# A state-space convolution with routed low-rank update: kernel numbers split into high and low parts before the skew, blocks reversed in time

## What is computed

```
P = dtA[:, :, None] * arange(L);  Cs = Cc * (exp(dtA) - 1) / A
K = 2 * Re(einsum('hn,hnl->hl', Cs, exp(P)))
y = irfft(rfft(u * mask) * rfft(K))[..., :L] + (u * mask) * D[:, None]
y = y * mask
```

## Time and profile before

| | us |
|---|---|
| runs | 608.7, 608.7, 610.63 |
| median | 608.7 |
| the profiled execution | 609.9 |
| its span in the profile | 608.1 |
| PE busy | 581.6 (96% of the span) |
| PEld, DVE busy | 529.0, 490.3 |
| POOL, ACT busy | 385.9, 317.2 |

### The profile page before, as it was taken

The page is one execution under the profiler, slowest core; times in us unless marked ns, Lnnn a source line. Parts: engine busy times, 40 slices in busy tenths (PEclk is TensorE's granted clock), DMA queues, the critical chain, the costliest instruction groups (busy, mean ns, idle before and its releaser), DMA issues.

```text
span 608.1 us, 13318 instructions
## 1 busy us (share of the span) xinstructions
PE 581.6 (96%) x3617; PEld 529.0 (87%) x3617; DVE 490.3 (81%) x1371; ACT 317.2 (52%) x1059; POOL 385.9 (63%) x520
## 2 busy tenths in 40 slices
PE   3589999999999999999999999999999999999996
PEld 3478999999999989999999999999999999999984
DVE  7768888887888888788888888888888888887875
ACT  3666754555465455546545554664555456445420
POOL 4668657666765766676575667657566765665430
PEclk9999999999999999999999999999999999999999
DMA  6212454454345344434534443453444345445422
GB/s 119 73 54 86 149 155 98 144 155 125 120 148 156 100 141 153 125 119 148 157 96 143 153 135 110 148 157 97 143 152 132 114 147 157 102 139 151 138 85 83
DMA packets 37582, 77.64 MB, mean 128 GB/s; under 512 B 12476, under 2 KB 20862, under 8 KB 37510
## 3 DMA queue, kind: packets, MB, share of 16 engines
q1 hardware_dynamic: 28358, 43.76, 28.8%
q10 hardware_dynamic: 9152, 33.03, 13.3%
HBM read 43.16 MB, written 33.62 MB: 126 GB/s over the span
## 4 chain that ended last, share of the span: by engine, by line
PE 92%; DVE 3%; ACT 2%; issue 1%; POOL 1%; DMA 0%; ACTq 0%; POOLq 0%
PE psYo L1060 20%; PE psZ L1080 19%; PE psO L1060 15%; PE psYe L1060 13%; PE psS L1060 11%; PE psO L1107 5%; PE psXe L1071 5%; PE psXo L1071 5%; PE psZ L1136 1%; DVE psS L918 0%; DVE ex L758 0%; DMA logs<-in_L_cond_log_dt_dram 0%; POOL both L465 0%; DVE ost L957 0%; ACT L577 0%
## 5 line engine op out<-in xcount | busy, mean ns | idle before, releaser
L504 POOL TENSOR_TENSOR Slo<-Sf,Shi 128x384 fp32r<-128x384 f32 x64 | 65.3, 1021 | 166.1 <-ACT Shi L651 166.1
L918 DVE SCALAR_TENSOR_TENSOR psS<-Sf,tab,psS 64x128 f32<-64x128 f32 x256 | 91.9, 359 | 48.1 <-ACT Sf L646 41.2
L1080 PE MATMUL psZ<-Wt,Y 128*128 128x136 f32 x1024 | 129.2, 279 | 0.0
L1080 PEld LDWEIGHTS psZ<-Wt,Y 128*128 128x128 f32 x1024 | 123.3, 190 | 0.1
L646 ACT ACTIVATE Sf<-psS 128x128 f32<-128x128 f32 x64 | 17.8, 277 | 200.3 <-PE psS L1060 200.3
L957 DVE TENSOR_TENSOR ost<-psO,xt 128x512 f32<-128x512 f32 x128 | 87.7, 690 | 1.2 <-PE psO L1060 1.1
L497 POOL TENSOR_TENSOR Xlo<-xeven,Xhi 128x512 fp32r<-128x512 f32 x64 | 82.9, 1295 | 0.0
L465 POOL TENSOR_TENSOR both<-coarse,fine 128x512 f32<-128x512 f32 x64 | 69.0, 1079 | 1.3 <-ACT fine L591 1.2
L941 DVE TENSOR_TENSOR wlo<-psZ,whi 128x128 fp32r<-128x128 f32 x64 | 18.7, 292 | 41.2 <-ACT whi L656 41.2
L1060 PE MATMUL psYo<-Xhi,Thi 128*128 128x512 f32 x128 | 51.2, 400 | 0.0
L1060 PE MATMUL psYo<-Xlo,Thi 128*128 128x512 f32 x128 | 51.1, 399 | 0.0
(11 more groups left out here) (193 smaller groups left out, 1522.2 us busy)
## 6 DMA issues: line engine op xcount, KB each, us to landing
xt<-in_x_dram SPq DMA_DIRECT2D x64, 512.0 KB, 4.9
out_dram<-ost ACTq DMA_DIRECT2D x63, 512.0 KB, 5.1
Traw<-kdram SPq DMA_DIRECT2D x64, 128.0 KB, 2.9
kdram<-krow SPq DMA_DIRECT2D x64, 1.0 KB
A_nat<-in_L_ffn_A_dram SPq DMA_DIRECT2D x1, 512.0 KB, 5.1
B_nat<-in_L_ffn_Bw_dram SPq DMA_DIRECT2D x8, 64.0 KB, 3.5
out_dram<-ost SPq DMA_DIRECT2D x2, 256.0 KB, 2.0
lens_i<-in_itok_B_dram SPq DMA_DIRECT2D x1, 64.0 KB, 5.0
```

The source lines that it names most:

```text
L504: pool.tensor_tensor(Slo[h.s2][:, :], Sf[h.s2][:, :], Shi[h.s2][:, :].bitcast(F32), ALU.subtract).then_inc(slo_done, 1)
L918: dve.scalar_tensor_tensor(psS[to, new], Sf[h.s2][fr, old], tab2[fr, BR, h.n:h.n + 1], psS[to, new], ALU.mult, ALU.add).then_inc(brought_d ...
L1080: last = pe.matmul(psZ[:, 0:NW], Y[:, j, c, :], Wt[:, 2 * c + j, :], start=(j == 0 and c == 0), stop=(j == 1 and c == NE - 1), skip_group_ ...
```

## The change

K is split into hi and lo while it is still two columns (`k_split`, ACT), all four columns are transposed, two DMAs write them into two rows of DRAM, and one DMA reads both, skewed, into one tile `T` (128x2x256, four buffers), which PE loads as it is. `t_hi` and `t_lo` are gone. Since nothing reads the skewed numbers backwards any more, the positions of the outputs stand reversed inside each block of 128. `g_hi` and `g_lo` read `Grev` forwards and `from_states` takes the halves of G the other way round, the mask counts positions downwards, and the weights of `project` are reversed once in the setup: `A_rev` by a copy on POOL, `route_rev` by one on ACT.

```diff
-        zeros = sb("zeros", [1, P])
+        zeros = sb("zeros", [2, P])
+        A_rev = sb("A_rev", [P, NB, P])
+        route_rev = sb("route_rev", [E, NB, P])
...
             def write_kernel(h):
                 need(sp, k_turned, h.n + 1)
                 need(sp, t_in[h.s2], h.half * 16)
-                sp.dma_start(bass.AP(kdram.tensor, h.s2 * (P + Q), [[G32, P // G32], [P, 2], [1, G32]]),
-                             krow[h.s2][0:P:G32, :, :]).then_inc(k_out[h.s2], 16)
+                for part in range(2):
+                    sp.dma_start(bass.AP(kdram.tensor, (h.s2 * 2 + part) * (P + Q),
+                                         [[G32, P // G32], [P, 2], [1, G32]]),
+                                 krow[h.s2][0:P:G32, part, :, :]).then_inc(k_out[h.s2], 16)
...
             def skew_kernel(h):
-                need(sp, thi_done, h.n - 1)
-                need(sp, tlo_done, h.n - 1)
-                need(sp, k_out[h.s2], h.half * 16 + 16)
-                sp.dma_start(Traw[h.s2][:, :],
-                             bass.AP(kdram.tensor, h.s2 * (P + Q), [[1, P], [1, Q]])
+                need(sp, y_mm, (h.n - 3) * 2)
+                need(sp, k_out[h.s2], h.half * 32 + 32)
+                sp.dma_start(T[h.s4][:, :, :].bitcast(F32),
+                             bass.AP(kdram.tensor, h.s2 * 2 * (P + Q), [[1, P], [P + Q, 2], [1, Q]])
                              ).then_inc(t_in[h.s2], 16)
...
+            pool.wait_ge(in_A, 16)
+            pool.tensor_copy(A_rev[:, :, :],
+                             A_nat[:, :].rearrange("p (c l) -> p c l", l=P)[:, :, ::-1]).then_inc(rev_done, 1)
             pool.wait_ge(g_set, 6)
             pool.wait_ge(tab_done, 1)
...
-            def t_hi(h):
-                need(act, t_in[h.s2], h.half * 16 + 16)
-                need(act, y_mm, (h.n - 1) * 2)
-                act.activation(Thi[h.s2][:, :, :].rearrange("p a b -> p (a b)"), Traw[h.s2][:, ::-1],
-                               ACT.Copy).then_inc(thi_done, 1)
+            def k_split(h):
+                need(act, kraw_done, h.n * 2 + 2)
+                need(act, k_turned, h.n - 1)
+                act.activation(kcol[h.s2][:, 0, :, 0:1], kraw[h.s2][:, :].rearrange("p (j a) -> p j a", a=1),
+                               ACT.Copy).then_inc(khi_done, 1)
+                need(act, khi_done, h.n + 1)
+                for j in range(2):
+                    act.activation(kcol[h.s2][:, 1, j, 0:1], kcol[h.s2][:, 0, j, 0:1].bitcast(F32), ACT.Identity,
+                                   scale=-1.0, bias=kraw[h.s2][:, j:j + 1]).then_inc(klo_done, 1)
...
             x_even(first[0])
+            act.wait_ge(in_rw, 16)
+            act.activation(route_rev[:, :, :], route_nat[:, :].rearrange("p (c l) -> p c l", l=P)[:, :, ::-1],
+                           ACT.Copy).then_inc(rev_done, 1)
             act.wait_ge(tabs_turned, 1)
...
             def turn_k(h):
-                need(dve, kcol_done, h.n * 2 + 2)
+                need(dve, klo_done, h.n * 2 + 2)
...
                 if head(2).there:
+                    b_lo(head(2))
                     turn_k(head(2))
-                    b_lo(head(2))
...
             def within(h, j):
-                need(pe, thi_done, h.n + 1)
-                need(pe, tlo_done, h.n + 1)
-                T = [(Thi[h.s2][:, j, :], Tlo[h.s2][:, j, :]) for j in range(2)]
+                need(pe, t_in[h.s2], h.half * 16 + 16)
+                K = [(T[h.s4][:, 0, j * P:(j + 1) * P], T[h.s4][:, 1, j * P:(j + 1) * P]) for j in (1, 0)]
...
-            pe.wait_ge(in_A, 16)
-            pe.wait_ge(in_rw, 16)
+            pe.wait_ge(rev_done, 2)
```

More of the change, by code:

```diff
@@ L521, in step @@
                     g_table(head(3))
-                if head(1).there:
-                    t_lo(head(1))
                 if head(3).there:
@@ L540, in _ @@
             angle_steps(parts[1])
-            t_lo(first[0])
             g_lo(first[1])
@@ L548, in _ @@
             weigh(parts[1])
-            t_lo(first[1])
             g_lo(first[3])
@@ L597, in g_hi @@
                 need(act, y_mm, (h.n - 3) * 2)
-                act.activation(Ghi[h.s4][:, :], Grev[h.s2][:, ::-1], ACT.Copy).then_inc(ghi_done, 1)
+                act.activation(Ghi[h.s4][:, :], Grev[h.s2][:, :], ACT.Copy).then_inc(ghi_done, 1)
             def m_matrix(h):
@@ L669, in step @@
                     b_hi(head(2))
+                    k_split(head(2))
                 if head(0).there:
@@ L673, in step @@
                     x_even(head(1))
-                    t_hi(head(1))
                 if head(3).there and not is_head(head(0), 1):
@@ L720, in _ @@
             b_hi(first[0])
+            k_split(first[0])
             g_hi(first[0])
@@ L726, in _ @@
             b_hi(first[1])
-            t_hi(first[0])
+            k_split(first[1])
             s_hi(first[0])
@@ L733, in _ @@
             b_hi(first[2])
+            k_split(first[2])
             g_hi(first[2])
@@ L736, in _ @@
             m_matrix(first[3])
-            t_hi(first[1])
             g_hi(first[3])
@@ L1119, in within @@
                 need(pe, y_masked, h.n * 2 - 1 + j)
[L1120 removed]
+                three(psY[j][:, :], [(K[0], X[j])] + [(K[1], X[0])] * j, True, False)
             def from_states(h):
@@ L1127, in from_states @@
                 for j in range(2):
-                    G = tuple(g[h.s4][:, j * P:(j + 1) * P] for g in (Ghi, Glo))
+                    G = tuple(g[h.s4][:, (1 - j) * P:(2 - j) * P] for g in (Ghi, Glo))
                     three(psY[j][:, P:512], [(G, (Shi[h.s2][:, :], Slo[h.s2][:, :]))],
@@ L1183, in _ @@
             turn_tables(pack1, psY[0], 4)
-            pe.wait_ge(in_A, 16)
-            pe.wait_ge(in_rw, 16)
+            pe.wait_ge(rev_done, 2)
             for c in range(NB):
                 cols = slice((c % 4) * P, (c % 4 + 1) * P)
-                pe.transpose((psO[1] if c // 4 else psZ)[:, cols], A_nat[:, c * P:(c + 1) * P], ident[:, :])
+                pe.transpose((psO[1] if c // 4 else psZ)[:, cols], A_rev[:, c, :], ident[:, :])
             for c in range(NB):
-                last = pe.transpose(psS[:, c * E:(c + 1) * E], route_nat[:, c * P:(c + 1) * P],
+                last = pe.transpose(psS[:, c * E:(c + 1) * E], route_rev[:, c, :],
                                     ident[0:E, 0:E])
```

49 lines of the change are left out of this document (21 added, 28 removed).

## The result

| | before | changed |
|---|---|---|
| median of the runs, us | 608.7 | 612.88 (612.22 to 613.07, four runs) |
| ratio | | 1.0059, interval 1.0038 to 1.0080 |
| the profiled execution, us | 609.9 | 613.03 |
| its span, us | 608.1 | 611.2 |
| PE, PEld, DVE busy, us | 581.6, 529.0, 490.3 | 583.0, 531.6, 493.9 |

The changed kernel is slower by 0.6%. POOL lost 43 us of work and PE gained nothing from it. The time, 612.9, lies outside the predicted range (607.2 to 611.3).

What follows compares the result with a forecast made beforehand. PE's own work was taken to bound the loop, its waits being single and in the setup. Terms 1.3 - 0.4 - 0.2 = +0.7 gave 610.6 for the profiled execution, less 1.2 = 609.4 us; range 607.2 to 611.3.

Steps and rivals of the forecast that it cites:

- 0 in all, never below 0: Loop: work taken off POOL and ACT gains nothing, the added work stays hidden from PE; 0 us, never a gain.
- The change gives PE the same matmuls of the same shapes: Loop: PE's matmuls keep shapes and order, so the loop can only lose, by making PE wait; no size beyond 0.
- The copy of A, +1.3: Setup: POOL's copy holds up DVE's chain of exponentials by about its own length; +1.3 us, ends 0 and +2.5.
- The first head, -0.4: First head: T lands without Thi and Tlo, so PE starts at 32.6 instead of 33.06; -0.4 us, ends -1.8 and +0.5.
- DVE now makes Blo first: Loop: DVE makes Blo, then transposes 128 columns instead of 64, perhaps 0.1 us more, covered by 0.64 us idle.
- The second head, -0.2: Second head: Thi and Tlo leave the queues of ACT and POOL, so the wait for gated values shortens by 0.2 us.
- The race at the first table: Setup: POOL's table starts before DVE's rho and is not held, giving back 0.9 us: 608.5; chance 0.16.
- rival 2: Setup: the copy of A costs DVE nothing, starting later or not holding it: 608.1 us; chance 0.10.
- Rival 3: Setup: the copy takes the two-input price of 2.5 us and the first head wins nothing: 611.2 us; chance 0.13.
- Rival 4: Loop: a split of 1.1 us or longer delays Shi past its slack; each further 0.1 us costs 6 us; chance 0.04.
- Rival 5, the clock: First head: after a shorter pause PE's clock might rise before 33 us, saving up to 2.4: 607.0 us; chance 0.07.
- From the profiled execution to the median, -1.2: Whole kernel: the profiled execution's 1.2 us above the median of 608.7 is taken off the forecast at the end.

Runs made afterwards that it cites:

- run 2: Changed kernel with Blo made before K's transpose in the setup's first three heads, and A reversed on ACT instead of POOL: 610.44 us, ratio 1.0016.
- run 1: Changed kernel with Blo made before the transpose of K's columns for the first three heads of the setup: 611.25 us, ratio 1.0034.
- run 13: Kernel before, whole, with 79 groups of 12 matmuls appended after its last product, moving operand addresses; first mark at 49.07 us, no total time given.
- run 8: Changed kernel with Blo first, A reversed on ACT, tiles at 64-byte multiples, and Mx and first state ahead of the second head's sines: 610.81 us.
- run 12: Changed kernel with Blo first, A reversed on ACT, kraw padded, plus six one-column ACT operations behind the split in each loop head: 657.07 us.
- runs 7 and 15: Changed kernel with Blo first and A reversed on ACT; then all tiles at 64-byte multiples (609.2 us), or kraw padded and operands 32 bytes off (609.72).
- run 4: Changed kernel with kraw padded from 2 to 16 columns: 609.83 us (one run).
- run 3: Kernel before with two unused tiles of the size of A_rev and route_rev: 609.26 us (one run).
- run 10: Kernel before with two unused two-column tiles where the changed kernel has kraw: 610.84 us, ratio 1.0016.

## Why the prediction was wrong

**The loop, "0 in all, never below 0": wrong, by 1.6 us.** The argument went over the waits, and every point of it held: no repeated wait, Shi in time, T hidden, whi and wlo in time (wlo ends at 307.27 and PE loads the first operand of `up` at 307.36, 0.09 us later, where it was 0.07). The first step that failed stands in front of it: "The change gives PE the same matmuls of the same shapes", from which their length was taken to be the same. It depends on where the operands lie too, and the change had moved them. It could also have gone the other way: with kraw at 16 columns the loop would have been 0.8 us shorter than before, so "never below 0" was wrong as well. No row shows this; the last sentence of the prediction's signs ("matmuls of another length in the loop than now") names it only as what would prove it wrong.

**The copy of A, +1.3: the mechanism right, the size 0.95.** DVE stood still under POOL's copy, as under Xlo in the earlier trace rows, and ACT's copy in run 2 takes the cost away. A copy of 1024 columns took 1.11 us, less than half the price by columns of Xlo (2.5) and less than the halved 1.3. The Trainium skill (GPSIMD Engine Reference, Performance versus the Vector engine) gives 1.8 cycles an element as the best case, 1.5 us as an estimate; the measured 1.11 is below it, and it decides.

**The first head, -0.4: the gain and its eater were both missed.** PE's `within` started at 33.07 against 33.06. Taking off the 0.95 of the copy, which comes first, the head won 0.94 and not 0.4, since T landed 3.1 us after its issue and not 3.6. But `bring`, which goes ahead of `within`, had become 0.79 us later. This is the second step that failed. "DVE now makes Blo first" is said of the loop, where it is so; in the setup the code keeps `turn_k` ahead of `b_lo`, and `turn_k` now waits for the split. The split's 0.7 us were counted on the way of T and not for who stands behind `turn_k` on DVE, so the sum has no term for Blo. The delay passed down to the states and the next inputs (2.0 us for Mx, 1.6 for issue), and by run 1 it was worth 1.55 us at the first mark. The first mark was late by 0.81 where the sum had +0.7, but that was luck: the profiled execution of the kernel before ran its first head at the pace of 1.2 GHz and the changed one at 2.4. Against run 13, the kernel before at 2.4, the changed kernel's mark is late by 2.2 us (51.31 against 49.07).

**The second head, -0.2.** One wait for the gated values (1.3 us) went, and others took its place; run 8 shows how they are handed on.

**Rivals.** The race at the first table didn't flip: the changed kernel has rho at 21.78 and POOL's table at 21.82 with 1.97 us, both 1 us later. The copy did cost, which ends rival 2. Rival 3's price for the copy (2.5) was too high; its time (611.2) came nearest and is still 1.7 us too low, for another reason. Rival 4 stayed away, with 0.5 us to spare, and is real beyond that (run 12). Rival 5, the clock: PE indeed worked at 2.4 GHz from 33.07 on (0.39 us for a product that took 0.63 until 36.61 before), and the gain was lost to the waits behind. But the shorter pause is not shown to be the cause: with the full pause of 1.84 us run 13 ran fast there too, and with pauses of 0.95 and 0.86 runs 7 and 15 ran slow. In the stretch from 42 to 50 us, after waits of 1.55 and 1.95 us, the granted clock was 0.79:

```profile
42.00:50.00 8.00, 7.40 (x37) 6.99 (x38) 4.98 (x16) 6.82 (x27) 4.93 (x10) 0.79 0.32 100
```

and the 16 products of the projection at 43.25 took 3.55 us instead of 2.0. In run 4 they took 2.0 after waits of 1.03 and 1.95 us.

**From the profiled execution to the median, -1.2.** The third step that failed: "I take the 1.2 off at the end" takes what the kernel before's profiled execution had above its median for something that the changed kernel's has as well. That one was only 0.15 us above its median, so this added 1.05 us to the difference of the medians. The spans of the kernel before, over all comparisons, lie in two groups, 606.7 to 607.1 and 607.7 to 608.4 us, and the profiled one is of the upper. The slow first head, worth 1.0 to 1.4 us at the first mark (50.50 against 49.51 in run 3 and 49.07 in run 13), is of the size of that distance and would explain it; the executions that make the median have no trace, so this is not shown.

**In sum**, 4.2 us against the forecast's 0.7, by the profiled executions: 1.6 from the step's length (not foreseen), 0.1 more in the setup (0.81 for 0.7), 0.7 from the clock at the end and 1.05 from the step to the medians. With the first heads at the same clock it reads otherwise: 1.6 from the step and 1.5 more than forecast in the setup (2.2 for 0.7, which is what Blo's place costs in run 1), which leaves 0.4 for the end and the rest.

**Small signs.** POOL's busy time fell to 342.7 (forecast about 340). ACT's did not fall by something but rose by 12.6 us: the split shows 0.72 us a head where Thi had 0.41. T landed after 3.8 us in the median (3.6), and x after 5.7 instead of 4.9, which cost nothing:

```profile
xt<-in_x_dram SPq DMA_DIRECT2D x64, 512.0 KB, 5.7
...
T<-kdram SPq DMA_DIRECT2D x64, 256.0 KB, 3.8
```

## What to carry to other kernels

Where PE is full and no wait repeats, a change can still cost some tenths of a per cent by moving the tiles that PE reads: before a small loss is put down to the edit, add an unused tile to the old kernel, or pad the new one, and time that. A wait that moves onto an operation holds up everything behind it in its queue, and the setup often has an order of its own: look up each place where the order is written, not the loop's alone. Work taken from engines that nobody waits for is worth nothing; here the change's whole gain lay in one head. And one profile shows one execution: where PE's products run at another pace than in the next profile of the same kernel, compare marks of like pace, or the difference goes to the wrong edit.

## What was not expected of the hardware

The spacing of the same fp32r product, with nobody waited for and all other engines idle, went from 226.5 to 236.8 ns with the start of its operands (run 13), while at 1.2 GHz a product of this shape is spaced by 425 to 427 ns (run 10's end). In the loop the fp32r products of 512 columns are mostly spaced by 224 to 238 ns, by their place in the step and the layout (the first of `within` by 315 to 325), and the fp32 ones by 109, 112 and 116 in the median (128, 129 and 136 columns) whatever the layout.

PE's pace in the first head differed between executions of the same instructions, 0.43 or 0.23 us from product to product, with 1.00 listed as granted in both (the kernel before and run 13).

The Trainium skill (TensorE: Matmul & The Clock Gate, Back-to-back issue gap) has 216 ns for the gap of a single product of 512 columns, as columns by 2.4 GHz and 2.5 ns, and its section "Step-by-step: what each phase is for" says that loading the next stationary operand takes no bandwidth from the running product. No product here reached 216, and the table shows that the start of the stationary operand alone makes 6 to 7 ns; the 427 ns at the lower clock are what the page gives.
